# Attention: the whole rotation on VectorE in the second head's probability tile, and the second head's outputs copied ahead of the first high parts

## What is computed

```python
def _rope(x):                       # rotates the first 32 of 64 channels
    x1, x2 = (xr[..., :half], xr[..., half:])
    xr = jnp.concatenate([x1 * cos - x2 * sin, x1 * sin + x2 * cos], -1)
    return jnp.concatenate([xr, xp], -1)

q = _rope(jnp.einsum('bsd,hdp->bhsp', x, Wq))
k = _rope(jnp.einsum('bsd,hdp->bhsp', x, Wk))
v = jnp.einsum('bsd,bhse,hedp->bhsp', x, gv, Wv)     # 8 experts, gates gv
att = jax.nn.softmax(jnp.einsum('bhsp,bhtp->bhst', q, k) / np.sqrt(P), axis=-1)
o = jnp.einsum('bhst,bhtp->bhsp', att, v)
return jnp.einsum('bhsp,bhse,hepd->bsd', o, go, Wo)  # 8 experts, gates go
```

## Time and profile before

| | |
|---|---|
| median of 3 timed runs | 4556.02 us (4555.58 to 4556.17) |
| the profiled execution | 4550.93 us |
| its span | 4549.1 us, mean granted clock 0.901 |
| TensorE busy | 3873.6 us (85%) |
| VectorE busy | 3483.8 us (77%) |
| GpSimd busy | 2705.4 us (59%) |
| ScalarE busy | 2037.9 us (45%) |

### The profile page before, as it was taken

One profiled execution on the slowest core, in us unless ns is written; L12 is line 12 of the kernel. 1 busy time (PEld: TensorE's weight loads), 2 busy tenths in 40 slices (PEclk: granted clock), 3 DMA queues, 4 the chain that ended last, 5 costly groups with the idle time before them and its releaser, 6 DMA issues. The chain is left out here.

```text
span 4549.1 us, 52321 instructions
## 1 busy us (share of the span) xinstructions
PE 3873.6 (85%) x16256; PEld 2698.3 (59%) x16256; DVE 3483.8 (77%) x3612; ACT 2037.9 (45%) x3761; POOL 2705.4 (59%) x1772
## 2 busy tenths in 40 slices
PE   6776766857666399999999999999999999999787
PEld 2232322323222277777777777777777777777676
DVE  5999999999999566666666666666666666666598
ACT  4544534435343144444444444444544544444443
POOL 2756656566476365665665666656655755665454
PEclk7786777868776699999999999999999999999899
DMA  1000000000000210010010000000100100000001
GB/s 37 0 10 14 10 19 19 9 14 9 23 9 10 76 62 14 14 39 9 14 39 9 32 21 14 35 14 14 39 9 14 39 9 14 19 14 9 34 28 42
DMA packets 48726, 97.83 MB, mean 22 GB/s; under 512 B 3570, under 2 KB 33138, under 8 KB 46228
## 3 DMA queue, kind: packets, MB, share of 16 engines
q1 hardware_dynamic: 47620, 92.94, 5.8%
q0 software_dynamic: 1040, 4.19, 0.2%
HBM read 80.34 MB, written 16.78 MB: 21 GB/s over the span
## 5 line engine op out<-in xcount | busy, mean ns | idle before, releaser
L723 DVE TENSOR_TENSOR_SCAN state<-dA,dBx 128x2048 f32<-128x2048 f32 x128 | 706.5, 5519 | 9.3 <-POOL y_part L309 4.3
L1015 POOL TENSOR_TENSOR qk_full<-vg 128x512 f32<-128x512 f32 x256 | 329.9, 1289 | 455.6 <-DVE vg L1330 455.6
L1230 ACT ACTIVATE prob<-ps_b,negmax 128x512 f32<-128x512 f32 x512 | 346.1, 687 | 549.3 <-DVE negmax L1336 549.3
L306 POOL TENSOR_TENSOR state<-state,c_copy 128x1024 f32<-128x1024 f32 x120 | 302.0, 2516 | 420.6 <-DVE state L723 420.6
L396 PE MATMUL ps_a<-xp_high,ident_r 33*128 33x512 f32 x256 | 163.3, 638 | 425.1 <-DVE dBx L713 399.7
L1330 DVE TENSOR_TENSOR vg<-ps_b,gates 128x1024 f32<-128x1024 f32 x256 | 313.6, 1225 | 255.0 <-PE ps_b L1072 251.2
L573 ACT ACTIVATE dA<-dt,a_neg 128x511 f32<-128x511 f32 x512 | 326.9, 711 | 398.3 <-DVE state L723 397.9
L1029 POOL TENSOR_TENSOR ogT_low<-prob,ogT_high 128x512 fp32r<-128x512 f32 x256 | 322.0, 1287 | 201.6 <-ACT ogT_high L1261 201.6
L1070 PE MATMUL ps_b<-wv_high,xT_high 128*128 128x512 f32 x1024 | 414.2, 404 | 0.0
L1070 PE MATMUL ps_b<-ogT_high,wo_high 128*128 128x512 f32 x1024 | 408.4, 399 | 0.0
L396 PEld LDWEIGHTS ps_a<-xp_high,ident_r 33*128 33x128 f32 x256 | 59.5, 232 | 583.2 <-DVE dBx L713 488.6
(11 more groups left out here) (232 smaller groups left out, 9658.0 us busy)
## 6 DMA issues: line engine op xcount, KB each, us to landing
xT<-xT_scratch SPq DMA_DIRECT2D x65, 512.0 KB, 3.2
wv<-in_wv SPq DMA_DIRECT2D x8, 1024.0 KB, 4.9
wo<-in_wo SPq DMA_DIRECT2D x8, 1024.0 KB, 6.9
x_in<-in_x SPq DMA_DIRECT2D x8, 512.0 KB, 4.6
x_a<-in_x SPq DMA_DIRECT2D x8, 512.0 KB, 5.3
x_scratch<-x_a SPq DMA_DIRECT2D x8, 512.0 KB, 2.9
xT_scratch<-x2T SPq DMA_DIRECT2D x8, 512.0 KB, 2.6
gates_scratch<-gate SPq DMA_DIRECT2D x8, 512.0 KB, 3.5
```

The source lines that it names most:

```text
L723: dve.tensor_tensor_scan(h[n % 2][:, :, :].rearrange("p c s -> p (c s)"), dA[n % 2][:, :, :].rearrange("p c s -> p (c s)"), dBx[n % 2][:, ...
L1015: pool.tensor_tensor(v4[:, at, :, :], vg[:, at, 0:4, :], vg[:, at, 4:8, :], ALU.add).then_inc(vsum_done, 1)
L1230: act.activation(prob[h][:, t, :], ps[:, score_bank(t) + h, :], ACT.Exp, bias=negmax[:, t, h:h + 1], accum_out=total[:, h, t:t + 1]).then_ ...
```

## The change

It does three things in stage_b. The tile `rot` becomes the second head's probability tile, so VectorE no longer waits for GpSimd's `low_outputs` ahead of `turn_raw`. The two GpSimd operations of `rotate` go to VectorE: the product with sin is now taken first, straight from PSUM, with a sin table whose rows are permuted beforehand, then the product with cos, then the shuffle of the sin product in place, then the sum. All four come ahead of the second head's `low_outputs`. And on ScalarE `keep_outputs(it, 1)` comes ahead of `high_outputs(it, 0)`.

```diff
--- before.py
+++ after.py
@@ -897,14 +897,14 @@
         probT = parts("probT", [P, RING, S])
 
         og = prob[0]
-        rot = prob[0]
+        rot = prob[1]
         ogT = parts("ogT", [P, EP, S])
 
         consts_loaded, consts_done, zero_done = sem("consts_b_loaded"), sem("consts_b_done"), sem("zero_done")
         tables_loaded, gates_loaded, acc_loaded = sem("tables_loaded"), sem("gates_loaded"), sem("acc_loaded")
         w_loaded, w_high, w_low = ({n: sem(f"{n}_{what}") for n in shapes} for what in ("loaded", "high_done", "low_done"))
         xT_loaded, xT_high, xT_low = sem("xT_loaded"), sem("xT_high_done"), sem("xT_low_done")
-        raw_psum, rot_done, sin_done, qk_done = sem("raw_psum"), sem("rot_done"), sem("sin_done"), sem("qk_done")
+        raw_psum, rot_done, qk_done = sem("raw_psum"), sem("rot_done"), sem("qk_done")
         qk_high, qk_low = sem("qk_high_done"), sem("qk_low_done")
         v_psum, vg_done, vsum_done = sem("v_psum"), sem("vg_done"), sem("vsum_done")
         v_high, v_low = sem("v_high"), sem("v_low")
@@ -997,16 +997,6 @@
                 pool.wait_ge(w_high[n], j * 2 + h + 1)
                 pool.tensor_tensor(w[n][1][:, h], w_in[n][:, h], w[n][0][:, h].bitcast(F32), ALU.subtract).then_inc(w_low[n], 1)
 
-            def rotate(it):
-
-                pool.wait_ge(tables_loaded, 32)
-                pool.wait_ge(rot_done, it * 2 + 2)
-                pool.tensor_tensor(rot[:, 2:4, :], rot[:, 2:4, :], sin[:, :, :], ALU.mult).then_inc(sin_done, 1)
-                pool.wait_ge(og_done, CREDIT + it * EP)
-                pool.wait_ge(vsum_done, CREDIT + it * VSUM)
-                pool.wait_ge(sin_done, it + 1)
-                pool.tensor_tensor(qk_full[:, :, :], rot[:, 0:2, :], rot[:, 2:4, :], ALU.add).then_inc(qk_done, 1)
-
             def sum_values(it, h, half):
 
                 at = slice(2 * half, 2 * half + 2)
@@ -1032,7 +1022,6 @@
                 low_wqk(0)
                 low_half(0, "wv", 0)
                 low_half(0, "wv", 1)
-                rotate(0)
 
             def pair_start(j):
                 low_half(j, "wo", 0)
@@ -1054,8 +1043,6 @@
                 if more_pairs:
                     low_half(j + 1, "wv", 0)
                     low_half(j + 1, "wv", 1)
-                if more or more_pairs:
-                    rotate(it + 1)
 
             pool.memset(out_gate[:, :, :], 0.0).then_inc(zero_done, 1)
             low_x(0)
@@ -1288,9 +1275,9 @@
                     high_probabilities(it, n)
                 high_gates(it)
                 keep_outputs(it, 0)
+                keep_outputs(it, 1)
                 high_outputs(it, 0)
                 high_outputs(it, 1)
-                keep_outputs(it, 1)
                 high_outputs(it, 2)
                 high_outputs(it, 3)
                 if more_pairs:
@@ -1312,9 +1299,18 @@
             def turn_raw(it):
 
                 dve.wait_ge(raw_psum, it * 2 + 2)
+                dve.tensor_tensor(rot[:, 2:4, :], ps[:, RAW:RAW + 2, :], sin[:, :, :], ALU.mult).then_inc(rot_done, 1)
+                dve.wait_ge(rot_done, it * 3 + 1)
                 dve.tensor_tensor(rot[:, 0:2, :], ps[:, RAW:RAW + 2, :], cos[:, :, :], ALU.mult).then_inc(rot_done, 1)
-                dve.stream_shuffle(rot[:, 2:4, :].rearrange("p a s -> p (a s)"), ps[:, RAW:RAW + 2, :].rearrange("p a s -> p (a s)"),
-                                   HALVES).then_inc(rot_done, 1)
+                turned = rot[:, 2:4, :].rearrange("p a s -> p (a s)")
+                dve.stream_shuffle(turned, turned, HALVES).then_inc(rot_done, 1)
+
+            def rotate(it):
+
+                dve.wait_ge(og_done, CREDIT + it * EP)
+                dve.wait_ge(vsum_done, CREDIT + it * VSUM)
+                dve.wait_ge(rot_done, it * 3 + 3)
+                dve.tensor_tensor(qk_full[:, :, :], rot[:, 0:2, :], rot[:, 2:4, :], ALU.add).then_inc(qk_done, 1)
 
             def low_qk(it):
                 dve.wait_ge(qk_high, it + 1)
@@ -1377,6 +1373,7 @@
 
             def start():
                 turn_raw(0)
+                rotate(0)
                 low_qk(0)
 
             def batch(it, j, b, more, more_pairs):
@@ -1397,8 +1394,8 @@
                 for p in range(EP):
                     gate_outputs(it, p)
                 if more or more_pairs:
-                    dve.wait_ge(oT_low0, it * EP + EP)
                     turn_raw(it + 1)
+                    rotate(it + 1)
                 for e in range(EP):
                     low_outputs(it, e)
                 if more or more_pairs:
@@ -1769,6 +1766,8 @@
     flat = np.ones((HP - NROT, S), np.float32)
     for name, parts in (("cos", (cos, cos, flat)), ("sin", (-sin, sin, 0 * flat))):
         table = np.tile(np.concatenate(parts), (2, 1))
+        if name == "sin":
+            table = table[np.concatenate([np.arange(half, NROT), np.arange(half), np.arange(NROT, HP)])[None, :] + HP * np.arange(2)[:, None]].reshape(P, S)
         out[name] = np.stack([table * np.float32(Q_SCALE), table], axis=1)
 
     row = np.arange(BLOCKS)[:, None] * 2 + np.arange(P)[None, :] // HP
```

## The result

The changed kernel takes 4617.56 us in the median of 4 runs (4609.29 to 4620.49), against 4555.8 us for the kernel before, run beside it. The ratio is 1.0133, with a 95% interval of 1.0115 to 1.015: slower by 62 us. The forecast was 4609 us. The profiled execution took 4620.05 us (span 4618.2), 69 us more than the profiled one of before.

A forecast was written before the change was run, and what follows sets the result against it. TensorE's fixed-order instruction list bounds the attention stage, so only its waits cost time. 41.6 (batches) + 14.7 (pair ends) - 2.4 (start) - 1 (last batch) = +52.9 us, forecast 4609 us, range 4575 to 4630.

The forecast's parts named there:

- Part 1: ScalarE copies the second head's outputs first; TensorE's wait at the third gate spreading goes, -0.84 us a batch.
- Part 2, the chain: Rotation on VectorE delays the first low part, stalling TensorE at project 4 by 1.50 us a batch.
- P: Start of project 0's first matmul on TensorE, from which the chain is timed; project 4 due at P + 5.60.
- The middle between the bounds: Net per-batch cost on VectorE's chain taken as 0.66 us, between 0.38 and 0.94, for unseen waits and SBUF shuffle.
- Pair ends: At seven pair ends GpSimd's value-weight split holds VectorE's sum 2.1 us, +14.7 us in all.
- rival (e): TensorE's new 1.24 us idle lowers its clock, +3 us a batch, 4800 us; chance 0.07 including anything above the range.
- The start: At the attention stage's start the rotation is on the path: new chain 5.04 us instead of 7.48, -2.4 us.
- The last batch: Between 0.8 and 1.9 us of TensorE's 1.88 us idle on the copy goes, no rotation there: -1 us.
- Rivals (a) to (d): Sum slips between splits, 4594 (0.25); waits also free, 4577 (0.10); faster SBUF shuffle, 4553 (0.04); that plus free waits, 4535 (0.04).
- (a): At pair ends VectorE's sum slips between GpSimd's two operations, if issued 0.3 us sooner: 4594 us; chance 0.25.
- The rule on SBUF's ports: VectorE instruction with two SBUF inputs and GpSimd instruction reading SBUF exclude each other throughout; counted against the sum on VectorE.
- The rule on the DRAIN: Semaphore between two VectorE operations costs nothing extra, giving near 4592; forecast went by rows instead, 1.27 against 1.14 us.

The follow-up runs named there:

- low_early: Changed kernel with VectorE's first low part between cos product and shuffle, the other three behind the shuffle, the sum last: 4497.52 us, ratio 0.9879.
- rot_alone: Changed kernel with ScalarE's old order, so only the rotation and its tile change: 4660.96 us, ratio 1.024.
- keep_alone: Kernel before with only the second head's output copy moved first on ScalarE, rotation as before: 4515.78 us, ratio 0.9914.
- tile_alone: Kernel before with only the rotation's tile changed to the second head's probability tile, dropping VectorE's wait for GpSimd: 4553.58 us, ratio 1.0001.
- wv_late: Changed kernel with GpSimd's two splits of the next pair's value weights waiting until VectorE's sum is done: 4591.57 us, ratio 1.0086.
- sum_last: Changed kernel with VectorE taking the rotation's sum after the four low parts instead of ahead of them: 4509.48 us, ratio 0.9906.

## Why the prediction was right

It was right in direction, in the place and, for the ordinary batch, to 0.02 us. The size was short by 9 us in the timed runs and by 16 us in the profiled one, most of it at the pair ends. The two differ because the profiled run lay 5 us under the median for the kernel before and 2.5 us above it for the changed one.

**Part 1** came as said: the copy starts when the last attend is done, and the wait is gone. Its worth was put at 0.84 us and is 0.82 by `low_early` and 0.85 by `rot_alone`. What the prediction did not say is that the full gain hangs on the tile: with the old tile 0.59 us stayed (`keep_alone`).

**Part 2, the chain.** From P: gating 0.19 (forecast 0.20), sin product 1.14 later (1.14), cos product 1.25 (1.27), shuffle 1.15 (1.15), sum 1.38 (1.36), first low part 1.14 (1.14). TensorE starts at P + 6.99 (7.00), its third matmul at P + 7.56 (7.57). The net was forecast at 0.66 us and is 0.68. The middle between the bounds was the right choice: a wait on the instruction just in front costs 0.1 us on VectorE (1.25 against 1.14), and the shuffle out of SBUF takes 1.34 us, as out of PSUM (1.32).

**Pair ends** were forecast at 2.1 us each and cost 3.4 to 4.7. The hold itself was right: the sum takes 3.17 instead of 1.23 us, 1.95 more, since GpSimd's operation ends when it does. What failed is the step in rival (e) that took the ordinary stall of 1.24 us for the new idle and asked about the clock only for that one. At pair ends the two effects add to 3.18 us, and the rows of before showed no idle time between 1.88 (no fall) and 7.2 us (fall); its trace has one more, 4.14 us ahead of 4273.15, with a fall. The runs fill it in: after 2.33 us the clock fell in six cases of seven, after 3.18 us in all seven, after 1.22 us in none of the ordinary batches. The single 1.88 us of before was thin ground too, since the same idle in `tile_alone` came with a fall. So the length of the idle time alone does not decide, and what else does stays open here. In the profiled execution the seven pair ends cost 28 us: 14 for the hold (14.7 forecast), and 14 for seven falls at 1.5 to 2.7 us, which the forecast lacked. `wv_late` takes hold and falls away together (26 us). Each alone is seen in `rot_alone`: at its first pair end the sum is held (2.33 us instead of 1.23) and the clock stays, and the other six give the price of a fall. That the falls differ in length from run to run would explain the spread of the changed kernel (4609 to 4620) against `wv_late` (4589 to 4593), but this was not tried separately.

**The start.** The chain itself is what was forecast: 5.08 us from VectorE's first product (1592.60) to ScalarE's first high part (1597.68), against 5.04. Only 1.4 of the 2.4 us show there, since that product began 1 us later than before, released by the transfer of the sin table and not by TensorE. This looks like chance: in the six other profiled kernels with the sin product in front, TensorE released it. The transfer took 13.1 us to land here and 10.7 to 12.3 in those six. Up to the first addition the profile gained 1.5 us, although the first batch has its 0.68 us too, because behind the start the clock was back at 1.00 sooner. From 1605 to 1608 it was 1.00, and 0.56 before. The last batch gave 0.5 us where 1 was forecast: three short waits of 0.2 to 0.4 us took the place of the 1.88.

Rivals (a) to (d) did not come about. Of (e) the part came that brings the clock down, but at the seven pair ends only, not in every batch. For (a) the sum would have had to be issued before GpSimd's second split began, at about 1930.26 (1927.88 and half of 4.76); it was issued at 1930.55. That is the 0.3 us by which the forecast, too, had it miss the gap.

**The rule on SBUF's ports** (the Trainium skill, "SBUF — State Buffer", "Who interferes with whom") gave the right account of the hold, with 3.17 against 1.23 us. **The rule on the DRAIN** (the Trainium skill, "VectorE: DVE Perf Modes") does not hold here to the last 0.1 us: three operations without a wait on the one in front follow at 1.14 to 1.15 us, one with such a wait at 1.25. The Trainium skill measured copies there, and the same section says that an operation that is not held starts earlier, which these rows do show.

## What to carry to other kernels

When work moves onto an engine, ask first who stands behind it in that engine's list, and measure the slack of that one: here, with the copy in front both times, the same four operations made the kernel 62 us slower ahead of the low parts and left it 44 us faster when one of them went behind. A wait that is worth nothing alone (the tile) may be what the next gain needs. `keep_alone` points that way, but the copy in front with the other tile and nothing else was not run. So test parts both alone and together. Add up the stalls that can fall into one place before asking whether an idle TensorE keeps its clock.

## What the runs showed of the hardware

- The clock of TensorE fell to 1.2 GHz after 2.33 us of idle in six cases of seven and after 3.18 us in seven of seven, and stayed after 1.22 us. After 1.88 us it stayed once (the kernel before) and fell once (`tile_alone`). At the pair end shown above it fell 1.3 us after the matmuls had begun again. At the third it was at 0.50 already from 2618.40 to 2619.00, before they began at 2619.11. A fall cost 1.5 to 2.7 us.
- A VectorE sum with two SBUF inputs that was issued during a GpSimd split took 3.17 us instead of 1.23 and ended 1.1 us behind the split, so it did its work only when GpSimd was through.
- A late weight costs TensorE before its matmuls run dry: in `sum_last` and `keep_alone` the matmuls show no idle time in the waits, yet the batch is 0.2 us longer, and the 0.4 us stand in the weight loads' row.
